# GpSimd's row moves wait for the landing of the second last move instead of for TensorE's progress

## The reference, cut to what matters

```
x = x + 0.5 * ffn(layernorm(x))
x = x + attn(layernorm(x))              # linear attention with rotary angles, a 5-tap convolution and a gate
x = x + 0.5 * ffn(layernorm(x))

ffn(x):
    shared = (silu(x @ shared_gate.T) * (x @ shared_up.T)) @ shared_down.T
    probs = sigmoid(x @ router_w.T + routing_bias)
    scores, indices = top_k(probs, 2);  scores = scores / sum(scores)
    # each token goes through 2 of 8 experts of width 256
    return shared + sum over its 2 experts e of  score_e * ((silu(x @ gate_w[e]) * (x @ up_w[e])) @ down_w[e])
```

## Time and profile before

| | us |
|---|---|
| median of 3 runs without the profiler (477.92 to 480.57) | 479.21 |
| span of the profiled execution, first to last instruction | 501.9 |
| TensorE busy in it | 462.0 |
| VectorE, ScalarE, GpSimd busy | 346.8, 271.0, 282.3 |

### The profile page before, as it was taken

The page is one execution under the profiler, slowest core; times in us unless marked ns, Lnnn a source line. Parts: engine busy times, 40 slices in busy tenths (PEclk is TensorE's granted clock), DMA queues, the critical chain, the costliest instruction groups (busy, mean ns, idle before and its releaser), DMA issues.

```text
span 501.9 us, 9741 instructions
## 1 busy us (share of the span) xinstructions
PE 462.0 (92%) x2975; PEld 382.8 (76%) x2975; DVE 346.8 (69%) x1064; ACT 271.0 (54%) x612; POOL 282.3 (56%) x290
## 2 busy tenths in 40 slices
PE   8979899989899999899989998999998998999896
PEld 4868678877788787688767877877776777888776
DVE  4999993333568865868889898899876532454355
ACT  5936135555476555476546664655464555565421
POOL 4148556665567245566636655686654555666562
PEclk9999999999999999999989999999999999999999
DMA  8981233253421334321132322114342253543323
GB/s 237 370 283 39 68 107 116 80 167 113 111 73 64 101 80 116 92 68 57 54 102 56 91 75 74 43 39 123 88 128 84 78 163 105 150 113 104 86 73 106
DMA packets 74353, 53.68 MB, mean 107 GB/s; under 512 B 9664, under 2 KB 68928, under 8 KB 74304
## 3 DMA queue, kind: packets, MB, share of 16 engines
q1 hardware_dynamic: 66112, 36.26, 24.4%
q0 software_dynamic: 8192, 16.79, 11.0%
HBM read 26.87 MB, written 26.15 MB: 106 GB/s over the span
## 4 chain that ended last, share of the span: by engine, by line
PE 50%; DVE 26%; issue 10%; ACT 6%; another core or an unknown queue 5%; DMA 2%; POOL 0%; SPq 0%; DVEq 0%; ACTq 0%; POOLq 0%
PE pool L888 12%; PE pool L877 6%; PE gu L843 5%; PE gu L845 5%; PE gu L844 5%; DVE X L1242 3%; PE gu L804 2%; DVE hs L1219 2%; PE pool L826 2%; DVE hs L1223 2%; PE gu L802 2%; DVE raw L1421 2%; PE gu L803 2%; DVE stats L1253 2%
## 5 line engine op out<-in xcount | busy, mean ns | idle before, releaser
L1176 POOL DMA_INDIRECT yg<-y_sorted,places x128 | 124.2, 970 | 94.3 <-PE gu L845 42.0
L1156 POOL DMA_INDIRECT x_sorted<-xn,places x128 | 129.7, 1013 | 83.3 <-PE gu L845 30.8
L1219 DVE TENSOR_TENSOR hs<-gs,gu 128x512 f32<-128x512 f32 x92 | 60.7, 663 | 89.4 <-ACT gs L1033 64.7
L1033 ACT ACTIVATE gs<-gu 128x512 f32<-128x512 f32 x124 | 72.1, 583 | 70.8 <-PE gu L804 24.8
L888 PE MATMUL pool<-w,hT 128*128 x708 | 99.3, 283 | 11.6 <-ACT hT L1039 9.7
L888 PEld LDWEIGHTS pool<-w,hT 128*128 128x128 f32 x708 | 87.6, 191 | 26.4 <-issue 23.0
L843 PE MATMUL gu<-w,xbt_hi 128*128 x177 | 81.8, 462 | 1.8 <-DVE xbt_lo L1205 1.5
L1039 ACT ACTIVATE hT<-pool 128x512 f32<-128x512 f32 x92 | 53.3, 580 | 36.2 <-PE pool L877 24.8
L845 PE MATMUL gu<-w,xbt_hi 128*128 x177 | 70.0, 396 | 0.0
L844 PE MATMUL gu<-w,xbt_lo 128*128 x177 | 69.9, 395 | 0.0
L1014 ACT ACTIVATE ys<-pool 128x256 f32<-128x256 f32 x92 | 34.5, 376 | 62.6 <-PE pool L888 34.2
(11 more groups left out here) (132 smaller groups left out, 786.8 us busy)
## 6 DMA issues: line engine op xcount, KB each, us to landing
xb<-x_sorted SPq DMA_DIRECT2D x85, 128.0 KB
y_sorted<-ys SPq DMA_DIRECT2D x85, 128.0 KB
x_sorted<-yg SPq DMA_DIRECT2D x6, 512.0 KB, 6.3
X<-x_dram SPq DMA_DIRECT2D x8, 256.0 KB, 4.8
x_sorted<-xn,places POOLq DMA_INDIRECT x128
yg<-y_sorted,places POOLq DMA_INDIRECT x128
out_dram<-X SPq DMA_DIRECT2D x8, 256.0 KB
raw<-gate_w_dram SPq DMA_DIRECT2D x4, 256.0 KB, 4.8
```

Source lines behind the costliest of these rows:

```text
L1033: nc.scalar.activation(dst, src, ACT.Silu).then_inc(silu_done, 1)
L1156: nc.gpsimd.indirect_dma_start(x_sorted[g], bass.IndirectOffsetOnAxis(places[g][:, k, t:t + 1], 0), xn[:, b, t % T], None).then_inc(scatte ...
L1176: nc.gpsimd.indirect_dma_start(yg[slot][:, k, t], None, y_sorted[g], bass.IndirectOffsetOnAxis(places[g][:, k, at:at + 1], 0)).then_inc(ga ...
L1219: v.tensor_tensor(hs[n % HB][:].rearrange("p (j i) -> p j i", j=2)[:, 0:k], gs[n % GB][:].rearrange("p (j i) -> p j i", j=2)[:, 0:k], bank ...
```

## The change

`pace` is replaced by `two_under_way`: a move waits until the move before the last one has landed, whatever kind that was. So at most two moves are under way. For this the semaphores of landings are split in two each, for moves of even and odd number; SyncE's first load of a group, VectorE's first add of a sample and ScalarE's normalization of layer 2 now wait for both halves. The planner, its `PACE` and the orders of all five engines are as before, and no instruction but waits is added, removed or moved.

```diff
-        scattered = [sem(f"scattered{g}") for g in groups]
-        gathered = [sem(f"gathered{b}") for b in range(B)]
+        scattered = [[sem(f"scattered{g}_{i}") for i in range(2)] for g in groups]
+        gathered = [[sem(f"gathered{b}_{i}") for i in range(2)] for b in range(B)]
...
                 if n == 0:
-                    once.wait_ge(scattered[g], 16 * 2 * tiles(g))
+                    for i in range(2):
+                        once.wait_ge(scattered[g][i], 16 * tiles(g))
...
-            def pace(*key):
-
-                half_through, through = plan.through(key)
-                wait(once, half_ready, half_through)
-                wait(once, gu_ready, through)
+            under_way = []
+
+            def two_under_way(landed, value):
+
+                if len(under_way) == 2:
+                    once.wait_ge(*under_way.pop(0))
+                under_way.append((landed, value))
...
-                pace("scatter", g, n)
+                two_under_way(scattered[g][n % 2], 16 * (n // 2 + 1))
                 nc.gpsimd.indirect_dma_start(
                     x_sorted[g], bass.IndirectOffsetOnAxis(places[g][:, k, t:t + 1], 0),
-                    xn[:, b, t % T], None).then_inc(scattered[g], 16)
+                    xn[:, b, t % T], None).then_inc(scattered[g][n % 2], 16)
...
-                pace("gather", l, b, n)
+                two_under_way(gathered[b][n % 2], 16 * (n // 2 + 1 + (0 if l == 1 else T)))
                 nc.gpsimd.indirect_dma_start(
                     yg[slot][:, k, t], None, y_sorted[g],
-                    bass.IndirectOffsetOnAxis(places[g][:, k, at:at + 1], 0)).then_inc(gathered[b], 16)
+                    bass.IndirectOffsetOnAxis(places[g][:, k, at:at + 1], 0)).then_inc(gathered[b][n % 2], 16)
...
                 if k == 0:
-                    once.wait_ge(gathered[b], 16 * 2 * T * (1 if l == 1 else 2))
+                    for i in range(2):
+                        once.wait_ge(gathered[b][i], 16 * T * (1 if l == 1 else 2))
```

## The result

The changed kernel takes 488.93 us (median of 4 runs, 486.38 to 491.09) against 479.33 us beside it (4 runs, 477.92 to 480.57). The ratio is 1.019, interval 1.0149 to 1.0231. The forecast of 477.6 us and its range to 482.5 us missed; the rival "the landing binds" had the sign and the mechanism.

A forecast was written before the change was run, and what follows sets the result against it. The prediction took TensorE, then VectorE, to bound the kernel; 1.7 us from earlier scatters, 0 from gathers and 0 for added waits gave a 500.2 us span, scaled to 477.6 us, range 473 to 482.5 us.

The forecast's parts named there:

- the landing binds: Rival, chance 0.15: the last 48 gathers fall behind if landings exceed 2.90 us; 481 to 484 us at 3.1 us.
- What bounds the kernel: Whole span: TensorE 50% and VectorE 26% of the chain; only 3 to 7 us hang on moves.
- The new wait, per move: GpSimd's moves: with two under way, one every 1.40 us, faster by 0.15 to 0.4 us each.
- What the earlier scatters give: TensorE's turns at groups 1, 2 and 5: loads come earlier, 1.7 us gained in sum.
- What the earlier gathers give: VectorE's adds and the kernel's end: counted as 0 gained, at most 1.3 us.
- What the change adds: Added waits for split semaphores on three engines: under 1 us together, 0 on the path.
- Sum: Whole kernel: span 501.9 - 1.7 = 500.2 us; scaled by 0.955 to the median, 477.6 us.
- Faster by more: Rival, chance 0.29: all waits for moves at turns, weight loads and adds come off, 472.7 us; half of it, 475.9.
- no gain at all: Rival, chance 0.12: loads come earlier, but TensorE waits the same time one step on, 479.2 us.
- the move itself gets longer: Rival, chance 0.04: moves stretch to one every 1.87 us, group starts 1, 2 and 5 wait longer, up to 493 us.

The follow-up runs named there:

- second execution of before: The kernel before, unchanged, profiled once more: span 479.3 us, 481.13 us without the profiler.
- experiment 5: Against the kernel before, scatters wait for the second last landing while gathers keep TensorE's pace: 480.29 us, ratio 1.000.
- 501.9 us execution: The first profiled execution of the kernel before, whose rows the prediction used: span 501.9 us.
- experiment 6: Three moves under way everywhere, but two before the 48 gathers of layer 3's samples 2 to 7, against the kernel before: 484.83 us, ratio 1.0095.
- experiment 1: Against the kernel before, semaphores of landings split by even and odd, TensorE's pace kept: 480.77 us, ratio 1.0004.
- experiment 7: Two moves under way everywhere, but three before the 48 gathers of layer 3's samples 2 to 7, against the kernel before: 482.66 us, ratio 1.0044.
- experiment 10: The changed kernel with one move under way instead of two, compared with the kernel before: 794.09 us, ratio 1.6542.
- experiment 3: The kernel before without its two pace calls, so moves wait for neither TensorE nor landings: 479.78 us, ratio 0.9995.

## Why the prediction was wrong

**What bounds the kernel.** That only 3 to 7 us hang on moves was a bound on the gain; I let it stand for a bound on the harm too. The 1.3 us that VectorE's adds idled for gathers were the warning: at those adds the gather already came last, so little slack was left. It was not nothing. In the second execution of before the adds of samples 3 and 4 idled 0.69 and 0.91 us, and yet samples 1 to 7 took as long as with no pace, where no add idles for a gather. In experiment 5 all adds together idled 2.5 us for gathers, at no loss (ratio 1.000). The changed kernel's 4.49 us at one add were far beyond that.

**The new wait, per move.** This is the step that failed. Its form held: a wait's end to the next start is 0.26 to 0.30 us, and two under way give (landing + 0.30) / 2. The landing was mis-sized: 2.41 us, from one gather of the chain, where the eight on the new chain took 3.15. By the formula that is 1.72 us a move, against 1.75 measured, 1.40 forecast and 1.56 before: the gathers that were to become faster became slower. The medians of all gathers are 2.6 us in either kernel, near my rows; but the stretch that decides is the one with the long landings, and a wait lets every long one through to the pace. The Trainium skill, DMA: Bandwidth & Descriptors (Anatomy of one DMA — SWDGE (gpsimd) path), gives a DMA that GpSimd issues a fixed part of about 2.0 us, mostly completion. The medians of 2.3 and 2.5 us with one move under way lie 0.3 and 0.5 us above it. By that figure alone, an estimate, two under way would come at (2.0 + 0.30) / 2 = 1.15 us, under the 1.26 at which GpSimd issues: it would have shown no loss at all.

**What the earlier scatters give.** Right in kind. Group 1's 24 scatters start from 59.90 to 93.20, 1.45 us a move (before 1.64, from 63.52 to 101.27), group 5's last at 381.00 instead of 383.59, and TensorE waits for no load at its turns. The term was 1.7 us from the 501.9 us execution; in the second one only 0.7 us stood there to be won, and experiment 5, which keeps this part alone, gains nothing that can be told (ratio 1.000).

**What the earlier gathers give.** I counted 0 to 1.3 us, and a few lines on that VectorE's idle time (69% busy) would cover them. They came later, not earlier, so a term of the sum that I had as a gain or nothing was a cost: 4.3 us at the late gathers (experiment 6), the rest in layer 1. The idle time did not cover it: VectorE takes its list in order, and `hs` stands behind the add.

**What the change adds.** Right: experiment 1 puts the split semaphores at 1.0004.

**Sum.** The factor 0.955 from span to median carried an unusual execution along; in all others the time is the span and 1.8 us.

**The rivals.** "The landing binds" had the mechanism and the main place right: the last 48 gathers, where the chain's landings of 3.15 us lie above its threshold of 2.90. Layer 1, where experiment 7's trace falls behind, it did not name. I gave it 0.15 because its price needed long landings and I had two short rows. Its own price for 3.1 us, 481 to 484, was too low as well: it let up to 2.8 us of slack at the end take a part, but the delay enters at samples 2 to 4 and is handed on by every later add (6.6 us late at the last one). "Faster by more" and "no gain at all" fall with the result; "the move itself gets longer" falls with mean times of 975 and 1012 ns against 978 and 1023 before.

## What to carry to other kernels

A wait for the landing of the n-th last move sets a pace of (landing + restart) / n; compare it with the needed pace at the longest landings of the busiest stretch, not at a median, and count all moves in the queue, not only the last ones. Here two were too few and three were free (ratio 0.9998). Where a consumer idles even a little for a transfer, little slack is left: find out when the next engine needs what stands behind the consumer in its engine's order, and price a delay of the transfer from there on in full. Here 0.69 us of idle time at an add were covered and 4.49 were not.

## What the runs showed of the hardware

- An indirect move of 128 rows by GpSimd lands 2.3 us (scatter) or 2.5 us (gather) after its start in the median with one under way (experiment 10). With two it is 2.3 and 2.6 us, with as many as GpSimd issues 2.3 and 2.8 us (experiment 3): more under way lengthens a gather a little and raises the pace much.
- With a stand of TensorE of 2.84 us came 6.7 us at half its clock, most of them behind it; with one move under way, where TensorE is busy for 65% of the span, its mean clock is 0.814.
